# The clamp of the square sums on POOL, and the merge of the local heads with its addition ahead of the second maxima

## The chip, the cores and the metric

The kernel runs on one core of one Trainium2 chip. The time is that of the device for one execution, in microseconds (us). The core has five engines that run their own instruction streams and meet through semaphores: PE (TensorE, matmuls), DVE (VectorE), ACT (ScalarE), POOL (GpSimd) and SP (SyncE, which here only issues DMAs). PE writes to PSUM, POOL reads and writes only SBUF.

## The reference

The input is 16 sequences of 512 tokens with 128 channels. A first attention (16 heads of 8 channels, causal, with rotary positions) is added to the input. Then come two layers of a local transformer: 8 heads of 64 channels that look at their own and the previous window of 64 tokens, and a gated MLP. What bears on the change is the local attention's normalisation of queries and keys and what follows it:

```
def l2norm(t):
    return t / jnp.clip(jnp.linalg.norm(t, axis=-1, keepdims=True), 1e-12)
...
q = l2norm(q) * qs
k = l2norm(k) * ksc
q, k = rotary_xpos(q, k)
o = local_attention(q, k, v)
o = o.transpose(0, 2, 1, 3).reshape(b, n, INNER)
x = x + o @ wo
h = shift_token(x)
```

The kernel takes the norm as (max(sum of squares, 1e-24)) to the power -0.5. The maximum is "the clamp".

## The kernel before, in words

**Work and slots.** Two sequences (lanes) form a pair, and there are 8 pairs, numbered 0 to 7. The local layers work on tiles of 128 tokens: 2 layers x 2 lanes x 4 tiles = 16 tiles per pair, 128 in all. Each engine's program is a loop over slots `s` = 0 to 15 of a pair, written out by hand, and slot `s` holds work of several tiles in different stages: the local scores of tile `s`, the output projection ("merge") and the addition of tile `s-1`, the transposes of queries and keys of tile `s+1`, the rotation on POOL of tile `s+2` and the projection and square sums of tile `s+3`. Beside it the slot carries the first attention of a later pair. Two bodies ahead of pair 0 fill this pipeline; in pair 7 and the second half of pair 6 it runs dry.

**The first attention in a slot.** `attention_step(s, pos)` with `pos` 0 to 5 stands at six places of a slot on PE, DVE and ACT. On PE a step first issues the score matmuls from which DVE takes the row maxima (L587, into one PSUM bank), and then the score matmuls of a head six heads back, whose exponentials ACT takes (L600 and the mask L602, into another bank). There is one bank for each: L587 of a step waits until DVE has read the maxima of the step before (`maxed`), and L600 until ACT has read the step before (`exped`). The steps are 512, 384 + 128, 256 columns wide and then the same again. DVE reads the maxima at L977 (with a short read of the accumulator behind each). "The second maxima" are those of `pos` 1.

**The places that the change touches.**
- DVE, `norms(m)`: L1029 sums the squares of 16 heads (128x1024 to 128x16, `ss`), L1032 clamps them in place. L1029 waits for POOL's power of the tile before, since `ss` is one buffer.
- POOL, `over_norms(m)`: L1408 raises `ss` to -0.5 into `inv`, once DVE's L1012 (`unit_heads`, which writes `QN`) has used the old `inv`. Behind it stand the rotation L1386, L1397 (twice), L1403, then the normalisation of a tile for the MLP (L1378, L1414, L1417). In even slots the four small instructions of `maxima_parts` (L1367 to L1373) come first, for which PE waits with L622; in slots 1 and 9 `next_normalise` and in slots 7 and 15 `first_normalise` are added.
- ACT, `squares(m)`: L1221 writes `SQ` once the clamp of the tile before is done.
- PE, `merge(m)`: L786 multiplies the transposed heads `OT` (copied by ACT at L1235) by the output weights, into `m_ps`.
- DVE, `add_heads(m)`: L1048 adds the residual to it. When it is done, SP moves half of the channels by one token (`shift_tokens`, DMA `XN<-Z`), for which L1058 waits.
- Around them on PE: L699 projects queries and keys, L554 transposes (`turn_*`), L819 and L828 are matmuls of the MLP in even slots, L801 and L810 in odd ones, L751 applies the local weights, L725 and L734 are the local scores. On DVE L1076 multiplies the gates ahead of L828, L1039 divides the local output (`ON`), L949, L953 and L957 belong to the rotary embedding of the first attention, L1089 adds the last residual, L1019 and L1022 take the maxima of the local scores at the start of a slot.

Of the kernel before, what the change touches and what calls it, by code (L numbers as in the profile page):

```python
# [170 lines left out]
def build(nc, t, out):  # L171
    with ExitStack() as ctx:
# [218 lines left out]
        def past(sem, value):  # L391

            return (made, N_MADE) if isinstance(value, int) and value <= 0 else (sem, value)
# [153 lines left out]
        def _(pe):  # L547
# [28 lines left out]
            def body(i, slots):  # L576
# [76 lines left out]
                def attention_step(s, pos):  # L653
                    h, c = step_at(s, pos)
                    if s % 2 == 0 and pos == 2 and unit_in(i, s // 2 + 10):
                        turn_maxima(s, s // 2 + 10)
                    if s % 2 and pos == 0 and unit_in(i, (s + 17) // 2):
                        values(s, (s + 17) // 2)
                    if s % 2 and pos == 4 and unit_in(i, (s + 17) // 2):
                        heads_out((s + 17) // 2)  # L660
                    if head_in(i, h):
                        scores_max(h, c)
                    if head_in(i, h - BEHIND):
                        scores_exp(h - BEHIND, c)
# [172 lines left out]
                for s in slots:  # L837
                    z, two = s // 8, later(i, 2)
                    a = s % 2 and piece_in(i, (s - 3) // 2)
                    b = s % 2 == 0 and piece_in(i, (s - 4) // 2)  # L840
                    p = (s - 3) // 2 if s % 2 else (s - 4) // 2
                    if isinstance(i, int) and i == -2 and s == 8:
                        pe.wait_ge(consts, 16 * N_CONST)
                        for e in range(RING):
                            pe.wait_ge(*past(ones_in[e].sem, 16))
                    if tile_in(i, s):
                        scores(s)
                    attention_step(s, 0)
                    if tile_in(i, s - 1):
                        turn_o(s - 1)  # L850
                    if tile_in(i, s + 3):
                        project_qk(s + 3)
                    attention_step(s, 1)
                    if tile_in(i, s - 1):
                        merge(s - 1)
                    attention_step(s, 2)
                    if tile_in(i, s):
                        turn_p(s)
                    if a:
                        half_turn(p, s)  # L860
                    if b:
                        ups(p, s)
                    attention_step(s, 3)
                    if tile_in(i, s + 1):
                        turn_qk(s + 1)
                    if s % 8 == 2 and lives(i, 2):
                        maxima_over(s)
                        next_project(two, z, 0)
                    if s % 8 == 4 and lives(i, 2):
                        maxima_over(s)  # L870
                        next_project(two, z, 3)
                    if s % 8 == 6 and lives(i, 1):
                        merged_turn(z)
                    attention_step(s, 4)
                    if a:
                        gates(p)
                    if tile_in(i, s):
                        attend(s)
                    if b:
                        down(p)  # L880
                    if tile_in(i, s + 1):
                        project_v(s + 1)
                    if a:
                        last_chunk(p)
                    if s % 8 == 2 and lives(i, 2):
                        next_project(two, z, 1)
                    if s % 8 == 6 and lives(i, 1):
                        merged_project(z)
                    if s == 12 and lives(i, 1):
                        if lives(i, 2):  # L890
                            pe.wait_ge(*past(roped.sem[1], roped.at(two, 4)))
                        else:
                            maxima_over(s)
                        first_turn(0)
                    if b and half_of(p)[0] < L - 1:
                        turn_half(p)
                    attention_step(s, 5)
                    if s % 8 == 1 and lives(i, 2):
                        heads_over(s)
                        if z:  # L900
                            pe.wait_ge(*past(v1_ready.sem[0], v1_ready.at(two, 1)))
                        next_turn(two, z)
                    if s % 8 == 3 and lives(i, 2):
                        heads_over(s)
                        next_project(two, z, 2)
                    if s % 8 == 5 and lives(i, 2):
                        heads_over(s)
                        next_values(two, z)
                    if s == 15 and lives(i, 1):
                        heads_over(s)  # L910
                        first_turn(1)
# [4 lines left out]
        def _(v):  # L916
# [53 lines left out]
            def body(i, slots):  # L970
# [23 lines left out]
                def attention_step(s, pos):  # L994
                    h, c = step_at(s, pos)
                    if head_in(i, h):
                        row_maxima(h, c)
# [28 lines left out]
                def norms(m):  # L1026
                    v.wait_ge(*past(sq_done.sem, sq_done.at(i, m + 1)))
                    v.wait_ge(*past(inv_ready.sem, inv_ready.at(i, m)))
                    v.tensor_reduce(ss[:, :], SQ.rearrange("p (h e) -> p h e", e=E2), AX.X,  # L1029
                                    ALU.add).then_inc(ss_sum.sem, 1)  # L1030
                    v.wait_ge(*past(ss_sum.sem, ss_sum.at(i, m + 1)))
                    v.tensor_scalar(ss[:, :], ss[:, :], 1e-24, None, ALU.max).then_inc(ss_ready.sem, 1)  # L1032

                def over_sums(m):
                    v.wait_ge(*past(o_mm.sem, o_mm.at(i, m + 1)))
# [55 lines left out]
                for s in slots:  # L1091
# [13 lines left out]
                        next_low(two, z, 0)  # L1105
                    if s % 8 == 6 and lives(i, 2):
                        next_low(two, z, 1)
                    attention_step(s, 1)
                    if tile_in(i, s - 1):
                        add_heads(s - 1)  # L1110
                    attention_step(s, 2)
                    if s % 8 == 3 and lives(i, 2):
                        next_rest(two, z, 0)
# [38 lines left out]
        def _(a):  # L1152
# [20 lines left out]
            def body(i, slots):  # L1173
# [43 lines left out]

                def squares(m):
                    a.wait_ge(*past(raw_ready.sem, raw_ready.at(i, m + 1)))
                    a.wait_ge(*past(ss_ready.sem, ss_ready.at(i, m)))  # L1220
                    a.activation(SQ, RAW[m % 2], ACT.Square).then_inc(sq_done.sem, 1)  # L1221

                def exps(m):
# [102 lines left out]
        def _(g):  # L1326
# [32 lines left out]
            def body(i, slots):  # L1359
# [43 lines left out]
                    g.tensor_tensor(RC, RC, RS, ALU.add).then_inc(added.sem, 1)  # L1403

                def over_norms(m):
                    g.wait_ge(*past(ss_ready.sem, ss_ready.at(i, m + 1)))
                    g.wait_ge(*past(qn_ready.sem, qn_ready.at(i, m)))
                    g.tensor_tensor(inv[:, :], ss[:, :], nhalf[:, :], ALU.pow).then_inc(inv_ready.sem, 1)  # L1408
# [107 lines left out]
```

## Time and profile before

| | us |
|---|---|
| median of 3 runs | 2443.62 |
| the runs | 2433.88 to 2451.03 |
| the profiled execution | 2439.99 |
| its span | 2438.2 |

The granted clock of TensorE was 0.98 of full speed in the mean. The chain of work that ended last is spread over many lines, with 38% of the span on PE, 21% on DVE, 14% on ACT and 13% on POOL; no line has more than 4%. A slot takes 16.2 to 19.3 us in pair 2, and the pattern of slot lengths comes back every 16 slots (about 283 us). From 2200 us on slots of 12.7 and 14.5 us alternate.

How to read the rows: PE's matmuls are pipelined, so their durations overlap. A start less the start before it tells more than a duration. DVE's and ACT's rows overlap by some tenths for the same reason. "[0.51 <-DVE nmax L977]" behind a row is the time that the engine stood idle before it and what released it.

### The profile page before, as it was taken

What the parts mean: (1) busy time and instruction counts of PE and PEld (TensorE: products, weight loads), DVE (VectorE), ACT (ScalarE), POOL (GpSimd) and SP (SyncE); (2) the same over time, 40 slices, a digit from 0 to 9 for tenths busy, and PEclk for the clock granted to TensorE, in tenths of its full rate; (3) what the DMA queues carried; (4) which work ended last, traced back from release to release, by engine and by line L of the source; (5) the groups of instructions that cost most, each with busy time, mean ns of one, the idle gap of its engine ahead of it and who ended that gap; (6) DMA issues with size and microseconds to landing.
All of it is one profiled execution on the core that took longest, in us unless ns stands there. A gap on an engine that the chain in (4) does not pass through costs nothing.

```text
span 2438.2 us, 55022 instructions
## 1 busy us (share of the span) xinstructions
PE 2153.6 (88%) x20736; PEld 1447.8 (59%) x20736; DVE 1763.4 (72%) x4632; ACT 1553.0 (64%) x2510; POOL 1773.9 (73%) x1615
## 2 busy tenths in 40 slices
PE   4887899899999989998999999999899999988886
PEld 1444566665666666665666656666566666665654
DVE  4766777787777877788777777778777777666653
ACT  1445666676676667666766766766676667765553
POOL 2126768787777868787686777878787778788882
PEclk9999999999999999999999999999999999999997
DMA  4222121121212111121112112121121211111110
GB/s 138 65 66 54 40 53 49 44 59 45 57 37 60 52 46 49 48 59 46 49 49 59 44 45 58 33 64 51 39 51 47 60 48 36 25 32 27 28 25 23
DMA packets 115081, 119.56 MB, mean 49 GB/s; under 512 B 31945, under 2 KB 88054, under 8 KB 114818
## 3 DMA queue, kind: packets, MB, share of 16 engines
q1 hardware_dynamic: 114818, 116.04, 18.2%
q8 instruction: 167, 2.74, 0.5%
q14 instruction: 96, 0.79, 0.1%
HBM read 55.96 MB, written 20.97 MB: 32 GB/s over the span
## 4 chain that ended last, share of the span: by engine, by line
PE 38%; DVE 21%; ACT 14%; POOL 13%; issue 11%; DMA 1%; SPq 1%; ACTq 0%; DVEq 0%; POOLq 0%
PE ps L734 4%; PE ps L645 4%; POOL inv L1408 4%; DVE ps L977 4%; PE ps L554 4%; PE ps L828 3%; DVE nm L1019 3%; PE ps L587 3%; DVE ss L1029 3%; PE ps L712 3%; PE ps L600 2%; PE ps L567 2%; ACT PT L1190 2%; PE ps L810 2%; PE ps L819 2%
## 5 line engine op out<-in xcount | busy, mean ns | idle before, releaser
L977 DVE CUSTOM_DVE_ANT_0 ps<-ps,causal 128x512 f32<-128x512 f32 (+3 forms) x1024 | 492.4, 506 | 328.3 <-PE ps L587 322.3
L1408 POOL TENSOR_TENSOR inv<-ss,nhalf 128x16 f32<-128x16 f32 x128 | 377.7, 2950 | 394.0 <-DVE QN L1012 394.0
L1190 ACT ACTIVATE PT<-ps 128x512 f32<-128x512 f32 (+1 forms) x768 | 409.1, 536 | 352.5 <-PE ps L602 349.8
L587 PE MATMUL ps<-KA,QA 72*128 72x512 bf16 (+3 forms) x1024 | 275.1, 311 | 77.1 <-DVE nmax L977 72.9
L1397 POOL TENSOR_TENSOR RS<-RAW,rot 128x512 f32<-128x512 f32 x256 | 319.9, 1271 | 0.0
L1403 POOL TENSOR_TENSOR RC<-RC,RS 128x1024 f32<-128x1024 f32 x128 | 300.9, 2351 | 18.4
L600 PE MATMUL ps<-QA,KA 75*128 75x512 bf16 (+3 forms) x1024 | 286.8, 306 | 27.8 <-ACT PT L1190 26.0
L1386 POOL TENSOR_TENSOR RC<-RAW,rot 128x1024 f32<-128x1024 f32 x128 | 307.9, 2405 | 0.0
L1019 DVE TENSOR_REDUCE nm<-ps 128x8 f32<-128x1024 f32 x128 | 156.4, 1222 | 119.3 <-PE ps L734 119.3
L699 PE MATMUL ps<-wqkv,ZT 128*128 128x512 f32 x512 | 241.9, 595 | 0.0
L587 PEld LDWEIGHTS ps<-KA,QA 72*128 72x128 bf16 x1024 | 96.4, 100 | 235.3 <-DVE nmax L977 142.4
L1249 ACT COPY V_odd<-ps 128x512 f32<-128x512 f32 x128 | 75.0, 586 | 233.6 <-PE ps L712 232.1
L1029 DVE TENSOR_REDUCE ss<-SQ 128x16 f32<-128x1024 f32 x128 | 155.7, 1217 | 72.5 <-POOL inv L1408 65.5
L602 PE MATMUL ps<-causal_t,identb 128*128 128x128 bf16 x1024 | 200.9, 222 | 0.0
L1225 ACT ACTIVATE PX<-PX 128x1024 f32<-128x1024 f32 x128 | 136.5, 1067 | 54.8 <-DVE PX L1022 54.1
L600 PEld LDWEIGHTS ps<-QA,KA 75*128 75x128 bf16 x1024 | 101.0, 99 | 115.8 <-ACT PT L1190 64.7
L645 PE MATMUL ps<-PT,V 128*32 128x512 f32 (+3 forms) x2048 | 153.4, 440 | 9.1 <-DVE X L1003 2.9
L1022 DVE TENSOR_TENSOR PX<-ps,nm 128x1024 f32<-128x1024 f32 x128 | 156.7, 1224 | 4.4
L1012 DVE TENSOR_TENSOR QN<-RC,inv 128x1024 f32<-128x1024 f32 x128 | 156.5, 1223 | 0.0
L828 PE MATMUL ps<-w,G 128*128 128x128 f32 (+1 forms) x768 | 110.8, 297 | 44.8 <-DVE G L1076 44.8
L734 PEld LDWEIGHTS ps<-KT,QT 64*64 64x64 f32 x4096 | 114.3, 136 | 56.7 <-issue 56.7
L751 PE MATMUL ps<-V_even,PT 128*64 128x65 f32 x2048 | 147.2, 225 | 0.4
(122 smaller groups left out, 5304.9 us busy)
## 6 DMA issues: line engine op xcount, KB each, us to landing
V_even<-V_odd SPq DMA_DIRECT2D x256, 130.0 KB, 2.6
QA<-parts SPq DMA_DIRECT2D x192, 96.0 KB
KA<-parts SPq DMA_DIRECT2D x192, 96.0 KB
parts<-qkp SPq DMA_DIRECT2D x32, 384.0 KB, 3.5
X_next<-in_x SPq DMA_DIRECT2D x16, 256.0 KB, 3.1
X<-in_x SPq DMA_DIRECT2D x16, 256.0 KB, 2.9
x_kept<-X SPq DMA_DIRECT2D x16, 256.0 KB, 3.8
XR<-x_kept SPq DMA_DIRECT2D x32, 128.0 KB, 2.9
```

What stands on the lines that cost most here:

```text
L587: last = pe.matmul(dst[:, c0:c0 + w], QA[e][0:QK_ROWS, h % UNIT, qt * P:(qt + 1) * P], KA[e][0:QK_ROWS, h % UNIT, 0:w], start=True, stop=True)
L600: pe.matmul(dst[:, c0:c0 + w], KA[e][0:ROWS, h % UNIT, kt * P:(kt + 1) * P], QA[e][0:ROWS, h % UNIT, kt * P:S], start=True, stop=False)
L645: last = pe.matmul(a_ps[32 * n:32 * (n + 1), kt * P:S], V1[z][:, kt, h * VW:h * VW + 32], PT1[:, n, c0:c0 + w], start=(kt == 0), stop=(kt ...
L699: mm = pe.matmul(ps[:, w, :], ZT[z][:, tt * P:(tt + 1) * P], wqkv[:, l, w * INNER:(w + 1) * INNER], start=True, stop=True)
L977: ins = v.tensor_tensor_reduce(for_max(i, x)[:, c0:c0 + w], for_max(i, x)[:, c0:c0 + w], causal[:, S - w:S], -1.0, -NEG, ALU.add, ALU.min, ...
L1019: v.tensor_reduce(nm[:, :], blocks, AX.X, ALU.max, negate=True).then_inc(max_ready.sem, 1)
L1029: v.tensor_reduce(ss[:, :], SQ.rearrange("p (h e) -> p h e", e=E2), AX.X, ALU.add).then_inc(ss_sum.sem, 1)
L1190: a.activation(PT1[:, h % UNIT, c0:c0 + w], for_exp(i, x)[:, 0:w], ACT.Exp, scale=SCALE1).then_inc(exped.sem, 1)
L1386: g.tensor_tensor(RC.rearrange(heads, w=2, h=H2), RAW[m % 2].rearrange(heads, w=2, h=H2), rot[:, l, tt, 0, :, :].unsqueeze(2).to_broadcast ...
L1397: ins = g.tensor_tensor(turned[:, w, :, :, :], by_half[:, w, :, :, :], table[:, w, :, :].unsqueeze(1).to_broadcast([P, H2, 2, E2 // 2]), A ...
L1403: g.tensor_tensor(RC, RC, RS, ALU.add).then_inc(added.sem, 1)
L1408: g.tensor_tensor(inv[:, :], ss[:, :], nhalf[:, :], ALU.pow).then_inc(inv_ready.sem, 1)
```

## The change

The clamp moves from DVE's `norms` to POOL's `over_norms`, ahead of the power. It waits for the sum, and ACT's `squares` now waits for the sum too. PE's `merge(s - 1)` moves from behind `attention_step(s, 1)` to ahead of it, and DVE's `add_heads(s - 1)` does the same.

```
@@ PE, the loop over slots
-                    attention_step(s, 1)
                     if tile_in(i, s - 1):
                         merge(s - 1)
+                    attention_step(s, 1)
                     attention_step(s, 2)
@@ DVE, norms(m)
                     v.tensor_reduce(ss[:, :], SQ.rearrange("p (h e) -> p h e", e=E2), AX.X,
                                     ALU.add).then_inc(ss_sum.sem, 1)
-                    v.wait_ge(*past(ss_sum.sem, ss_sum.at(i, m + 1)))
-                    v.tensor_scalar(ss[:, :], ss[:, :], 1e-24, None, ALU.max).then_inc(ss_ready.sem, 1)
@@ DVE, the loop over slots
-                    attention_step(s, 1)
                     if tile_in(i, s - 1):
                         add_heads(s - 1)
+                    attention_step(s, 1)
                     attention_step(s, 2)
@@ ACT, squares(m)
-                    a.wait_ge(*past(ss_ready.sem, ss_ready.at(i, m)))
+                    a.wait_ge(*past(ss_sum.sem, ss_sum.at(i, m)))
@@ POOL
                 def over_norms(m):
+                    g.wait_ge(*past(ss_sum.sem, ss_sum.at(i, m + 1)))
+                    g.tensor_scalar(ss[:, :], ss[:, :], 1e-24, None, ALU.max).then_inc(ss_ready.sem, 1)
                     g.wait_ge(*past(ss_ready.sem, ss_ready.at(i, m + 1)))
```

The lines between the removed and the added ones of DVE and POOL move up by two in the changed kernel (L1048 becomes L1046). On PE, in an even slot, these are the instructions between the transposes of `ON` and the maxima of step 2, before:

```order
L554 MATMUL ps<-ident,ON 128x128 x4
L699 MATMUL ps<-wqkv,ZT 128x512 x2
L587 MATMUL ps<-KA,QA 128x384
L587 MATMUL ps<-KA,QA 128x128
L600 MATMUL ps<-QA,KA 128x384
L602 MATMUL ps<-causal_t,identb 128x128
L600 MATMUL ps<-QA,KA 128x128
L602 MATMUL ps<-causal_t,identb 128x128
L786 MATMUL ps<-wo,OT 128x128 x4
L622 MATMUL ps<-identb,nparts 128x128 x4
L587 MATMUL ps<-KA,QA 128x256
```

And now:

```order
L554 MATMUL ps<-ident,ON 128x128 x4
L699 MATMUL ps<-wqkv,ZT 128x512 x2
L786 MATMUL ps<-wo,OT 128x128 x4
L587 MATMUL ps<-KA,QA 128x384
L587 MATMUL ps<-KA,QA 128x128
L600 MATMUL ps<-QA,KA 128x384
L602 MATMUL ps<-causal_t,identb 128x128
L600 MATMUL ps<-QA,KA 128x128
L602 MATMUL ps<-causal_t,identb 128x128
L622 MATMUL ps<-identb,nparts 128x128 x4
L587 MATMUL ps<-KA,QA 128x256
```

The merge (L786) no longer stands between the maxima of step 1 and those of step 2. In an odd slot L622 is not there, and only L600 and L602 are left between them.

On POOL, from the small instructions of `maxima_parts` to the rotation, before:

```order
L1371 TENSOR_TENSOR nparts<-nres,unit 128x4x4
L1373 TENSOR_TENSOR nparts<-nres,nparts 128x4x4
L1408 TENSOR_TENSOR inv<-ss,nhalf 128x16
L1386 TENSOR_TENSOR RC<-RAW,rot 128x1024
L1397 TENSOR_TENSOR RS<-RAW,rot 128x8x2x32 x2
```

And now:

```order
L1369 TENSOR_TENSOR nparts<-nres,unit 128x4x4
L1371 TENSOR_TENSOR nparts<-nres,nparts 128x4x4
L1405 TENSOR_SCALAR ss<-ss 128x16
L1408 TENSOR_TENSOR inv<-ss,nhalf 128x16
L1384 TENSOR_TENSOR RC<-RAW,rot 128x1024
L1395 TENSOR_TENSOR RS<-RAW,rot 128x8x2x32 x2
```

The clamp (now L1405) stands directly ahead of the power, in front of the power's wait for `QN`.

## Rows read from the trace of the kernel before

**Rows 1.** The page: busy us (share of the span) and instructions of each engine
```profile
PE 2153.6 (88%) x20736; PEld 1447.8 (59%) x20736; DVE 1763.4 (72%) x4632; ACT 1553.0 (64%) x2510; POOL 1773.9 (73%) x1615
```

**Rows 2.** Groups by line: busy us, mean ns, idle before and releaser
```profile
L1408 POOL TENSOR_TENSOR inv<-ss,nhalf 128x16 f32<-128x16 f32 x128 | 377.7, 2950 | 394.0 <-DVE QN L1012 394.0
...
L1032 DVE TENSOR_SCALAR ss<-ss 128x16 f32<-128x16 f32 x128 | 119.3, 932 | 4.4
...
L1048 DVE TENSOR_TENSOR Z<-ps,Z 128x128 f32<-128x128 f32 x64 | 18.5, 290 | 21.2 <-PE ps L786 21.2
...
L1367 POOL TENSOR_TENSOR nparts<-nmax,unit 128x16 bf16<-128x16 f32 x64 | 13.7, 215 | 107.3 <-DVE nmax L977 107.3
```

**Rows 3.** The line of the clamp alone: ns min/median/max, first and last start
```profile
L1032 DVE TENSOR_SCALAR ss<-ss x128: 175/878/3462, 192.8 to 2364.7; 128x16 f32<-128x16 f32 x128
```

**Rows 4.** Waits: who waited for whom, us in total, times, longest
```profile
POOL inv L1408 <- DVE QN L1012: 394.0, 92, 8.6
```

**Rows 5.** Timeline, slot 14 of pair 2: start, us, engine, instruction [idle before]
```profile
1048.02 1.22 DVE L1032 TENSOR_SCALAR ss<-ss 128x16 f32<-128x16 f32 x1
...
1047.93 2.50 POOL L1397 TENSOR_TENSOR RS<-RAW,rot 128x512 f32<-128x512 f32 x2
...
1050.19 1.60 PE L828 MATMUL ps<-w,G 128*128 128x128 f32 x12 [0.84 <-DVE G L1076]
```

**Rows 6.** Timeline, slot 1 of pair 2, DVE, POOL and PE
```profile
816.22 3.46 DVE L1032 TENSOR_SCALAR ss<-ss 128x16 f32<-128x16 f32 x1
...
817.15 2.50 POOL L1397 TENSOR_TENSOR RS<-RAW,rot 128x512 f32<-128x512 f32 x2
...
821.49 0.28 PE L587 MATMUL ps<-KA,QA 72*128 72x256 bf16 x1 [1.66 <-DVE nmax L977]
```

**Rows 7.** Timeline, slot 13 of pair 2 (odd), PE, then DVE, then ACT
```profile
1024.86 0.22 PE L602 MATMUL ps<-causal_t,identb 128*128 128x128 bf16 x1
1024.92 1.11 PE L786 MATMUL ps<-wo,OT 128*128 128x128 f32 x8
1025.87 0.27 PE L587 MATMUL ps<-KA,QA 72*128 72x256 bf16 x1
1026.43 0.28 PE L600 MATMUL ps<-QA,KA 75*128 75x256 bf16 x1 [0.29 <-ACT PT L1190]
...
1024.78 0.57 DVE L977 CUSTOM_DVE_ANT_0 ps<-ps,causal 128x384 f32<-128x384 f32 x1 [0.82 <-PE ps L587]
...
1025.51 0.14 DVE L977 DVE_READ_ACCUMULATOR2_ANT nmax<- 128x1 f32 x1
...
1025.74 0.63 ACT L1190 ACTIVATE PT<-ps 128x512 f32<-128x512 f32 x1
```

**Rows 8.** The chain that ended last, the same slot: start, us, what
```profile
1026.43 0.28 PE ps L600
```

**Rows 9.** Timeline, slot 10 of pair 2, DVE, then PE
```profile
970.97 0.14 DVE L977 DVE_READ_ACCUMULATOR2_ANT nmax<- 128x1 f32 x1
...
971.17 0.28 PE L587 MATMUL ps<-KA,QA 72*128 72x256 bf16 x1
```

**Rows 10.** Timeline, slot 12 of pair 2, DVE, then POOL
```profile
1013.80 2.33 DVE L949 TENSOR_TENSOR rope_t<-rope_t,rope_s 128x512 f32<-128x512 f32 x1
...
1013.23 2.35 POOL L1403 TENSOR_TENSOR RC<-RC,RS 128x1024 f32<-128x1024 f32 x1
```

**Rows 11.** Timeline, slot 8 of pair 2, DVE, then PE
```profile
942.50 0.65 DVE L1032 TENSOR_SCALAR ss<-ss 128x16 f32<-128x16 f32 x1
943.07 0.21 DVE L1058 BATCH_NORM_STATS2 stats<-XN 128x6 f32<-128x64 f32 x1
...
944.11 1.60 PE L828 MATMUL ps<-w,G 128*128 128x128 f32 x12 [0.71 <-DVE G L1076]
```

**Rows 12.** Late slots: a piece of the chain (the clamp), then a row of POOL's timeline
```profile
2253.12 0.77 issue
...
2303.12 2.92 POOL L1408 TENSOR_TENSOR inv<-ss,nhalf 128x16 f32<-128x16 f32 x1
```

More of the change, by code:

```diff
@@ L852, in body @@
                         project_qk(s + 3)
-                    attention_step(s, 1)
                     if tile_in(i, s - 1):
                         merge(s - 1)
+                    attention_step(s, 1)
                     attention_step(s, 2)
@@ L1030, in norms @@
                                     ALU.add).then_inc(ss_sum.sem, 1)
-                    v.wait_ge(*past(ss_sum.sem, ss_sum.at(i, m + 1)))
-                    v.tensor_scalar(ss[:, :], ss[:, :], 1e-24, None, ALU.max).then_inc(ss_ready.sem, 1)
                 def over_sums(m):
@@ L1107, in body @@
                         next_low(two, z, 1)
-                    attention_step(s, 1)
                     if tile_in(i, s - 1):
                         add_heads(s - 1)
+                    attention_step(s, 1)
                     attention_step(s, 2)
@@ L1219, in squares @@
                     a.wait_ge(*past(raw_ready.sem, raw_ready.at(i, m + 1)))
-                    a.wait_ge(*past(ss_ready.sem, ss_ready.at(i, m)))
+                    a.wait_ge(*past(ss_sum.sem, ss_sum.at(i, m)))
                     a.activation(SQ, RAW[m % 2], ACT.Square).then_inc(sq_done.sem, 1)
@@ L1405, in over_norms @@
                 def over_norms(m):
+                    g.wait_ge(*past(ss_sum.sem, ss_sum.at(i, m + 1)))
+                    g.tensor_scalar(ss[:, :], ss[:, :], 1e-24, None, ALU.max).then_inc(ss_ready.sem, 1)
                     g.wait_ge(*past(ss_ready.sem, ss_ready.at(i, m + 1)))
```

## The prediction

> **What bounds the kernel now.** The page comes first. PE is busy 88% of the span, and DVE, POOL and ACT 64 to 73% [rows 1], so no engine is full and each slot has its own last wait. A slot is the stretch between two starts of DVE's L1019. The reader should then look at the clamp, L1032. It handles 128x16 elements, yet it takes 932 ns in the mean [rows 2] and anything from 175 to 3462 ns [rows 3]. Its length depends on what it runs into. In slot 14 it starts at 1048.02 and ends at 1049.24, about where the first of POOL's two RS instructions ends (2.50 us from 1047.93, so half of it at 1049.18) [rows 5]. In slot 1 it starts at 816.22 and ends at 819.68, when POOL's RS pair, begun at 817.15, ends at 819.65 [rows 6]. So the clamp waits for POOL to let go, sometimes for one instruction and sometimes for three.
>
> The Trainium skill (SBUF — State Buffer, "SBUF: two separate sides") says that DVE and GpSimd share a port pair that one instruction holds to its end while the other blocks. Slot 14 agrees. In slot 1 the rule would free the clamp at 817.15, where RS begins, so the clamp would cost 0.93 us there, and taking it away could return no more than that instead of the 1.66 used below. The forecast would be 6 x 0.73 = 4.4 us higher, 2441.7.
>
> The chain of waits then says which slots feel DVE at all. In the odd slots but 1 and 7 it runs through ACT, whose exponentials follow PE's scores [rows 7, 8]. In slots 2 and 10 it runs through PE. In slots 6, 8 and 14 it runs through L1029, L1032, L1058 and the gates into PE's L828. In slots 7 and 8 POOL is the chain until PE's L622.
>
> **Change 1, the clamp leaves DVE.** DVE loses 128 x 932 ns = 119 us of busy time [rows 2], but only what a waiting engine gets counts. I take it by slot, for one pair (16 slots).
> - Slot 1: the clamp holds DVE for 3.46 us, and PE stands idle 1.66 us ahead of L587 because of it [rows 6]. PE can recover no more than that: 1.66.
> - Slots 6 and 14: the clamp costs 1.1 us, but PE's idle time ahead of L828 is 0.84 [rows 5]: 0.84 each, 1.68 (slot 6 repeats the pattern of 14).
> - Slot 8: 0.57 from the clamp's start (942.50) to that of L1058 (943.07), less than PE's idle 0.71 [rows 11]: 0.57.
> - Slots 0, 4 and 12: some 0.2 each. In slot 12 it goes nowhere: L949, which reads two SBUF tensors, waits until POOL's L1403 is over (15.58) and ends at 16.13, whenever it came [rows 10]. POOL's place there is set by QN, ahead of both edits. I take slots 0 and 4 alike: 0.
> - Slots 2 and 10 and the other odd ones: PE or ACT is the chain: 0.
>
> Gain per pair 1.66 + 1.68 + 0.57 = 3.9 us. The full pattern runs in pairs 0 to 5: 23.4 us.
>
> In the end of the program (from 2088 us, without the first attention's maxima) POOL and DVE alternate on the chain. In nine even slots the clamp stands on it with 0.9 us, from 2133 to 2365 us; its longest piece, here at 2253.12, is 0.77 [rows 12].
>
> **Change 2, the clamp on POOL.** The trace has no such instruction. Two rows of the same 128x16 shape on POOL bound it: 215 ns for a multiplication and 2950 ns for the power [rows 2]. Since a maximum is simple arithmetic, I take the first, with 0.08 of waiting for its own semaphore: 0.3. Where POOL waits for QN ahead of the power, which happens 92 of 128 times and 394 us in all [rows 4], the clamp runs inside that wait, since the sums were ready one slot earlier. If that cover were gone, it would cost 0.3 x 92 = 28 us at most. In 36 slots POOL does not wait, as at 2303.12 [rows 12]. The nine late slots are among them, where power, sums and gates follow each other: 0.9 - 0.3 = 0.6 each, a gain of 5.4 us. In slot 1 the 0.3 lies within the 1.8 us that PE's idle time leaves of the clamp's 3.46. The new wait on `ss_sum` holds up the power and the rotation behind it, but the sum comes before it by nearly a slot. ACT's squares wait for the sum instead of the clamp, and that was never their last wait.
>
> **Change 3, the merge ahead of the second maxima on PE.** The merge takes 0.95 us of PE (1024.92 to 1025.87) [rows 7]. In an odd slot PE comes to this place without a pause. Before, the scores of step 1 ended at 1025.08, and ACT, busy until about 1025.8, took them at 1025.74 [rows 7]. Now they end at 1026.03, so ACT loses 0.3. The larger loss is the next step. L587 of step 2 waits until DVE has read step 1 out of the same bank. That read took 0.87 (1024.78 to 1025.65), and the merge used to cover it. Now the read starts 0.95 later, at 1025.73, and ends at 1026.60; L587 starts at 1026.68 and L600 behind it at 1026.80, against 1026.43 [rows 7]. This L600 stands on the chain [rows 8]: +0.37, and ACT runs without a pause after it, so it goes through. That makes six slots (3, 5, 9, 11, 13, 15) x 0.37 = 2.2. In slot 1 QN delays DVE anyway: +0.28. In slot 7 POOL covers it: 0.
>
> In an even slot PE waits 0.5 ahead of step 1 and the merge fills part of that, but DVE is later still.
>
> **Change 4, the addition ahead of the second maxima on DVE.** It takes 0.29 [rows 2], some 0.25 from start to start. In slot 10 step 1 is read until 971.11 and PE starts step 2 at 971.17 [rows 9], so the two meet with nothing to spare and the addition puts PE back by 0.25. The same holds for slots 2, 6 and 14: 1.0 per pair. In 0, 4 and 12 it is absorbed like the gain, and in 8 POOL covers it. The tokens get to SP's queue earlier by 0.3 to 0.8, but DVE hardly waits for that shift. Cost of changes 3 and 4 per pair: 2.2 + 0.28 + 1.0 = 3.5, over six pairs 21.0, and in the thinner pair 6 1.5 (slots 1, 3 and 5 at 0.37, and 0.4 for the even ones).
>
> **Sum.** -23.4 - 5.4 + 21.0 + 1.5 = -6.3 us. The profiled execution took 2439.99 (span 2438.2), 3.6 under the median of the runs, 2443.62. Against the median: **2437.3 us**, 0.3% less.
>
> **The rivals.**
> - A, the gain alone: the moved merge costs nothing, since PE and ACT make up 0.4 us elsewhere in the slot. For it: PE has idle time in each slot. Against it: in the odd slots it lies ahead of the chain. 2443.6 - 23.4 - 5.4 = 2415.
> - B, the stall moves on (the slower side): the other DVE instructions with two SBUF inputs, L949 and L1089, now start a little earlier against POOL's row of instructions and miss a hand-over as the clamp did in slot 1. If one of them per pair waits 3.46 more [rows 6], that is 6 x 3.46 = 20.8: 2437.3 + 20.8 = 2458. It decides from 1.05 us per pair on (6.3 / 6). Against it: DVE arrives there within 0.1 of its old time, since gain and cost cancel.
> - C, the cost alone: PE's idle times of [rows 5, 6] have a second cause right behind the clamp, so the 23.4 and the 5.4 fail and the cost stays, with 0.3 x 9 for the clamp on POOL: 2443.6 + 22.5 + 2.7 = 2469.
> - D, the clamp is as slow on POOL as the power: 2.65 more in six slots 1 and nine late ones: 2437.3 + 15 x 2.65 = 2477. Against it: 215 ns for four other kinds of simple arithmetic of this shape.
>
> **Numbers.** The forecast gets 0.50, A 0.14, B 0.14, C 0.08, D 0.04; 0.10 is left for what I do not see, on both sides. Own range of the forecast: 2428 to 2446. Over all cases: 2418 to 2462, which leaves out most of A, C and D. A measurement of this kernel tells about 1% from no change, that is 2419 and 2468. Faster by over 1% 0.13 (nearly all of A), slower by over 1% 0.10 (D and half of C), within 1% 0.77.
>
> **What would show it.** In the profile after: DVE busy 119 us less; a clamp of about 0.2 us on POOL; slot 1 shorter by 1.4 us; PE's waits for DVE ahead of L828 nearly gone; but PE waiting ahead of step 2 for DVE in the odd slots, and ACT's exponential of step 2 about 0.4 us later after slot start. The forecast is wrong if the odd slots keep their length (A), or if L949 or L1089 grow in the mean (B).

## The result and the profile after

| | before | after |
|---|---|---|
| median of four runs each, us | 2447.32 | 2417.89 |
| lowest to highest | 2433.88 to 2452.00 | 2410.79 to 2421.13 |
| profiled execution (span) | 2439.99 (2438.2) | 2418.14 (2416.4) |

The ratio is 0.9885, with a 95% interval of 0.9838 to 0.9932: 1.15% faster. On the chip of the first experiments it was 0.9844 (0.9813 to 0.9876). The forecast of 2437.3, 0.3% faster, had the direction but a quarter of the size. It was worked out from a median of 2443.62, without the fourth run of the kernel before (2452.00). The time lies outside the forecast's own range (2428 to 2446), 0.1 under the lower end of the range over all cases (2418 to 2462) and next to rival A. A gain of over 1% had been given a chance of 0.13.

The page after, busy us of each engine, answers to [rows 1]:

```profile
PE 2140.1 (89%) x20736; PEld 1463.9 (61%) x20736; DVE 1698.7 (70%) x4504; ACT 1561.1 (65%) x2510; POOL 1826.3 (76%) x1743
```

DVE has 128 instructions less but only 65 us less to do, not 119. POOL has 52 us more. The groups by line (busy us, mean ns, idle before and releaser) answer to [rows 2]:

```profile
L1408 POOL TENSOR_TENSOR inv<-ss,nhalf 128x16 f32<-128x16 f32 x128 | 378.7, 2959 | 324.6 <-DVE QN L1012 320.0
...
L953 DVE TENSOR_TENSOR rope_s<-rope_t,qkp 128x512 f32<-128x512 f32 x32 | 66.4, 2074 | 1.4 <-ACT qkp L1160 1.4
...
L1405 POOL TENSOR_SCALAR ss<-ss 128x16 f32<-128x16 f32 x128 | 40.0, 313 | 0.0
```

And the clamp's line alone (ns min/median/max), which answers to [rows 3]:

```profile
L1405 POOL TENSOR_SCALAR ss<-ss x128: 247/256/1225, 197.5 to 2351.8; 128x16 f32<-128x16 f32 x128
```

The clamp takes 0.26 us on POOL in the median, near the 0.22 of a multiplication. Eight of the 128 take 1.1 to 1.2, so the mean is 0.31. Of the 55 us of DVE time that did not vanish, 44 have gone to L953, which reads two SBUF tensors: it took 0.69 us before and now takes 2.07 in the mean. L1089 (now L1087) has grown from 1.07 to 1.32 in the mean, 8 us in all, and L949 has shrunk from 1.34 to 1.21.

Slot 1 of pair 2 after (timeline, start, us; DVE, POOL, then PE) answers to [rows 6]:

```profile
809.05 1.22 DVE L1029 TENSOR_REDUCE ss<-SQ 128x16 f32<-128x1024 f32 x1 [1.18 <-POOL inv L1408]
810.19 0.22 DVE L1056 BATCH_NORM_STATS2 stats<-XN 128x6 f32<-128x64 f32 x1
...
805.69 0.25 POOL L1405 TENSOR_SCALAR ss<-ss 128x16 f32<-128x16 f32 x1
806.02 2.93 POOL L1408 TENSOR_TENSOR inv<-ss,nhalf 128x16 f32<-128x16 f32 x1
...
813.58 0.28 PE L587 MATMUL ps<-KA,QA 72*128 72x256 bf16 x1
```

L1056 (L1058 before) follows the sum at once where 3.46 us lay between. PE's L587 has lost its idle time of 1.66. The power starts 0.33 after the clamp does. PE's idle time ahead of L828 in slots 6, 8 and 14 of this pair is gone too. Over the whole trace PE's wait for the gates ahead of L828 is halved and not nearly gone, 21.4 us after 44.8.

Slot 13 of pair 2 after (PE, DVE, ACT) answers to [rows 7]:

```profile
1016.91 1.05 PE L786 MATMUL ps<-wo,OT 128*128 128x128 f32 x8
1017.80 0.38 PE L587 MATMUL ps<-KA,QA 72*128 72x384 bf16 x2
...
1019.20 0.28 PE L587 MATMUL ps<-KA,QA 72*128 72x256 bf16 x1 [0.68 <-DVE nmax L977]
1019.32 0.28 PE L600 MATMUL ps<-QA,KA 75*128 75x256 bf16 x1
...
1018.08 0.29 DVE L1046 TENSOR_TENSOR Z<-ps,Z 128x128 f32<-128x128 f32 x1 [1.56 <-PE ps L786]
1018.28 0.56 DVE L977 CUSTOM_DVE_ANT_0 ps<-ps,causal 128x384 f32<-128x384 f32 x1
...
1019.87 2.61 DVE L953 TENSOR_TENSOR rope_s<-rope_t,qkp 128x512 f32<-128x512 f32 x1
...
1018.57 0.60 ACT L1188 ACTIVATE PT<-ps 128x512 f32<-128x512 f32 x1
```

This is the new wait of the prediction's change 3. The second L587 now waits 0.68 us for DVE, where the merge stood before. The chain that ended last (start, us, what) runs through it:

```profile
1017.08 0.91 PE ps L786 x8
...
1018.08 0.29 DVE Z L1046
1018.37 0.47 DVE ps L977
...
1019.20 0.30 PE ps L587
```

Merge, addition, maxima of step 1, matmuls of step 2: each waits for the one before it. Over the whole trace the waits of PE for DVE's maxima (us, times, longest) have grown, before and after:

```profile
PE ps L587 <- DVE nmax L977: 72.9, 116, 3.9
...
PE ps L587 <- DVE nmax L977: 111.8, 147, 1.7
```

The slots of pair 1, in us between two starts of L1019, from the timelines of four kernels (two of them are experiments below):

```
slot            0    1    2    3    4    5    6    7    8    9   10   11   12   13   14   15   sum
before       16.6 17.8 16.5 18.2 19.3 18.5 18.4 16.2 17.6 17.3 16.5 18.4 18.8 18.5 18.2 16.6 283.5
after        16.6 16.0 16.6 18.7 19.4 18.8 17.7 16.6 16.5 17.4 16.7 18.8 18.6 18.8 17.6 16.8 281.4
clamp only   15.2 16.9 17.3 18.1 19.4 18.5 17.5 16.2 17.2 17.0 16.6 18.5 18.5 18.5 17.6 16.3 279.3
moves only   16.6 17.4 17.0 18.8 19.4 18.8 18.4 16.6 17.0 17.7 17.2 18.8 18.8 18.8 18.2 16.9 286.3
```

The change shortens slots 1, 6, 8 and 14 and lengthens the other odd ones by 0.1 to 0.5, 2.1 us less in all (in pair 2: 283.1 to 282.0, from the starts 783.38 and 1065.34 of after). Yet the two traces differ by 21.8 us in span. The rest lies in single pairs: 5.2 us in pair 0, 6.1 in pair 3, 2.4 in pair 4, 2.3 in pair 6, 3.9 in pair 7.

Two things set the longer pairs of the kernel before apart. In slot 15 of pair 3 a clamp takes 3.45 us, as in the slots 1; and TensorE's clock falls more often in some pairs. It is granted at 1.00 of full speed (2.4 GHz) for most of the time and falls to 0.50 (1.2 GHz) for stretches of 3.4 us, some of them twice as long. These rows show slot 4 of pair 3 and slot 4 of pair 4 in the trace before. First come the two windows with their length, the busy time of each engine and the granted clock (the third figure from the end), and then PE's rows:

```profile
1161.00:1165.00 4.00, 4.00 (x49) 2.04 (x42) 3.67 (x5) 0.96 (x3) 0.00 (x0) 1.00 0.03 10
1448.40:1451.70 3.30, 3.30 (x40) 1.75 (x40) 1.46 (x2) 0.87 (x2) 0.00 (x0) 0.50 0.26 90
...
1160.03 1.10 PE L734 MATMUL ps<-KT,QT 64*64 64x128 f32 x32
1161.06 2.36 PE L645 MATMUL ps<-PT,V 128*32 128x512 f32 x32
...
1448.21 1.94 PE L734 MATMUL ps<-KT,QT 64*64 64x128 f32 x32
1450.08 3.15 PE L645 MATMUL ps<-PT,V 128*32 128x512 f32 x32
```

The first slot takes 19.3 us and the second 20.2. Here are the eight pairs of four kernels (16 slots, 15 in pair 7), in us, with the number of stretches at half clock that begin there in brackets:

```
pair             0          1          2          3          4          5          6          7
before       282.0 (2)  283.5 (0)  283.1 (0)  287.4 (1)  285.7 (2)  283.3 (0)  256.3 (2)  211.5 (4)
after        276.8 (1)  281.4 (1)  282.0 (1)  281.3 (1)  283.3 (1)  283.5 (1)  254.0 (1)  207.6 (5)
clamp only   274.3 (0)  279.3 (0)  280.7 (1)  279.6 (0)  279.6 (0)  280.3 (0)  252.7 (1)  204.8 (4)
moves only   286.2 (3)  286.3 (0)  290.2 (2)  289.4 (1)  291.6 (3)  287.6 (2)  262.3 (2)  207.1 (2)
```

Each of the seven stretches in pairs 0 to 6 of the trace before comes with, or a few us behind, an idle time of PE of 1.65 to 3.88 us. Three of the seven follow a clamp of 3.45 us: in slot 1 of pair 0, in slot 15 of pair 3 and in slot 1 of pair 4. The same idle time does not always bring one. In both slots 4 above, PE stood idle for 2.35 us shortly ahead of L734. Nor does each stretch cost time: that of pair 1 after leaves slot 4 at 19.4 us.

### The profile page after: what moved, and what is told of

Same layout as the page of the kernel before. It is cut to its first block, busy times and chain, and to the rows that moved or that the text cites. A ratio compares the mean times of both kernels' runs of the same rounds, so it can differ in the third digit from the quotient of the medians.

```text
span 2416.4 us, 55022 instructions
## 1 busy us (share of the span) xinstructions
PE 2140.1 (89%) x20736; PEld 1463.9 (61%) x20736; DVE 1698.7 (70%) x4504; ACT 1561.1 (65%) x2510; POOL 1826.3 (76%) x1743
## 4 chain that ended last, share of the span: by engine, by line
PE 50%; DVE 20%; POOL 14%; issue 10%; ACT 4%; DMA 1%; SPq 0%; DVEq 0%; POOLq 0%; ACTq 0%
DVE ps L977 6%; PE ps L554 6%; PE ps L645 5%; PE ps L734 4%; PE ps L751 4%; PE ps L587 4%; PE ps L712 4%; PE ps L828 3%; DVE nm L1019 3%; POOL inv L1408 3%; PE ps L699 3%; PE ps L600 3%; PE ps L567 2%; PE ps L819 2%; PE ps L810 2%
## 5 line engine op out<-in xcount | busy, mean ns | idle before, releaser
L587 PE MATMUL ps<-KA,QA 72*128 72x512 bf16 (+3 forms) x1024 | 274.7, 310 | 113.7 <-DVE nmax L977 111.8
L1395 POOL TENSOR_TENSOR RS<-RAW,rot 128x512 f32<-128x512 f32 x256 | 330.1, 1311 | 0.0
L1384 POOL TENSOR_TENSOR RC<-RAW,rot 128x1024 f32<-128x1024 f32 x128 | 302.7, 2365 | 0.0
L600 PE MATMUL ps<-QA,KA 75*128 75x512 bf16 (+3 forms) x1024 | 285.5, 304 | 10.6 <-ACT PT L1188 9.0
L1019 DVE TENSOR_REDUCE nm<-ps 128x8 f32<-128x1024 f32 x128 | 156.3, 1221 | 112.3 <-PE ps L734 112.2
L587 PEld LDWEIGHTS ps<-KA,QA 72*128 72x128 bf16 x1024 | 99.3, 100 | 208.8 <-DVE nmax L977 145.5
L602 PE MATMUL ps<-causal_t,identb 128*128 128x128 bf16 x1024 | 200.7, 222 | 0.0
L786 PEld LDWEIGHTS ps<-wo,OT 128*128 128x128 f32 x1024 | 134.1, 191 | 63.0 <-issue 57.4
L645 PE MATMUL ps<-PT,V 128*32 128x512 f32 (+3 forms) x2048 | 161.3, 458 | 8.5 <-ACT PT L1188 2.3
L600 PEld LDWEIGHTS ps<-QA,KA 75*128 75x128 bf16 x1024 | 101.2, 99 | 81.2 <-ACT PT L1188 27.4
L554 PE MATMUL ps<-ident,PX 128*128 128x128 f32 x1024 | 138.5, 280 | 12.1 <-ACT PX L1223 12.1
```

Source lines behind the costliest of these rows:

```text
L554: last = pe.transpose(dst[:, tt * P:(tt + 1) * P], src(tt), ident[:, :])
L587: last = pe.matmul(dst[:, c0:c0 + w], QA[e][0:QK_ROWS, h % UNIT, qt * P:(qt + 1) * P], KA[e][0:QK_ROWS, h % UNIT, 0:w], start=True, stop=True)
L600: pe.matmul(dst[:, c0:c0 + w], KA[e][0:ROWS, h % UNIT, kt * P:(kt + 1) * P], QA[e][0:ROWS, h % UNIT, kt * P:S], start=True, stop=False)
L645: last = pe.matmul(a_ps[32 * n:32 * (n + 1), kt * P:S], V1[z][:, kt, h * VW:h * VW + 32], PT1[:, n, c0:c0 + w], start=(kt == 0), stop=(kt ...
L1384: g.tensor_tensor(RC.rearrange(heads, w=2, h=H2), RAW[m % 2].rearrange(heads, w=2, h=H2), rot[:, l, tt, 0, :, :].unsqueeze(2).to_broadcast ...
L1395: ins = g.tensor_tensor(turned[:, w, :, :, :], by_half[:, w, :, :, :], table[:, w, :, :].unsqueeze(1).to_broadcast([P, H2, 2, E2 // 2]), A ...
```

## The experiments

All times are medians of the runs of one kernel, all ratios are against runs of the kernel before on the same chip. Experiments of one group shared a chip.

**Apart: the clamp and the moves.** The first kernel is the change without these two edits; the second is the kernel before with these two alone.

```
-                    attention_step(s, 1)
                     if tile_in(i, s - 1):
                         merge(s - 1)
+                    attention_step(s, 1)
...
-                    attention_step(s, 1)
                     if tile_in(i, s - 1):
                         add_heads(s - 1)
+                    attention_step(s, 1)
```

> Only the clamp moves to POOL (with ACT's changed wait); merge and addition stay behind the second maxima. The theory of the prediction (the clamp gains, the moves cost 3.5 us per pair): 21 us faster than the whole change, some 2400 us, ratio to before 0.978 to 0.983, and the odd slots 3, 5, 11 and 13 keep the 18.5 us or less of before. The rival (the moves are free or help): equal to the whole change, ratio 0.988 and above.

> Only the merge on PE and the addition on DVE move ahead of the second maxima; the clamp stays on DVE. The theory: 20 us slower than before, ratio 1.006 to 1.011, with PE waiting for DVE ahead of L587 in the odd slots 0.4 us longer. The rival (the moves are free or help): ratio 0.995 to 1.002.

> The whole change once more, on the chip of the other runs, to compare with them: both theories expect its first ratio again, 0.984 to 0.993.

Measured: the clamp only 2404.37 us, ratio 0.9799 (0.9770 to 0.9828); the moves only 2468.36, ratio 1.0070 (1.0044 to 1.0096); the whole change 2415.94, ratio 0.9844; before 2450.15. So the clamp brings 46 us and the moves take 18 where the clamp is on DVE and 12 where it is on POOL. The theory that the moves cost stands, and rival A, in which they are free, falls. The whole change is 12 us slower than its first half alone, where 21 were expected. Slots 3, 5, 11 and 13 keep their length with the clamp only, 18.1 to 18.5, and grow by 0.3 to 0.6 with the moves only. Waits in the second kernel:

```profile
PE ps L587 <- DVE nmax L977: 120.8, 150, 3.6
```

**The clamp's own cost on POOL.** On the order of the kernel with the clamp only:

```
 def over_norms(m):
     g.wait_ge(*past(ss_sum.sem, ss_sum.at(i, m + 1)))
-    g.tensor_scalar(ss[:, :], ss[:, :], 1e-24, None, ALU.max).then_inc(ss_ready.sem, 1)
-    g.wait_ge(*past(ss_ready.sem, ss_ready.at(i, m + 1)))
```

> Merge and addition as before, and no clamp at all: the maximum of the square sums with 1e-24 is left out of the computation, and the power follows the sum at once. It measures the clamp's own cost on POOL against the kernel with only the clamp moved. The theory (0.3 us, hidden in POOL's wait for QN in most slots): 3 to 6 us faster than that kernel. The rival (the clamp's wait and dispatch on POOL cost in every slot): 20 us or more faster than it.

Measured: 2393.07 us, ratio 0.9754 (0.9726 to 0.9782), 11 us faster than with the clamp on POOL. Both expectations missed: it is more than 3 to 6, and less than 20. One more kernel, meant to clamp and raise to the power in one instruction on POOL, gave no time. To see whether the clamp's length is what counts, the next one has it twice:

```
     g.tensor_scalar(ss[:, :], ss[:, :], 1e-24, None, ALU.max).then_inc(ss_ready.sem, 1)
+    g.wait_ge(*past(ss_ready.sem, ss_ready.at(i, 2 * m + 1)))
+    g.tensor_scalar(ss[:, :], ss[:, :], 1e-24, None, ALU.max).then_inc(ss_ready.sem, 1)
```

> The kernel with only the clamp moved, with the clamp twice on POOL, the second waiting for the first. The kernel without a clamp was 11 us faster than the one with it on POOL. The theory (0.34 us per clamp in the slots where POOL is late, the cause of those 11): 8 to 15 us slower than with one clamp, ratio 0.983 to 0.986. The rival (the 11 us came from how POOL's and DVE's instructions happen to meet, not from the clamp's length): within 4 us of one clamp or faster.

Measured: 2423.13 us, ratio 0.9892 (0.9866 to 0.9918), 19 us slower than with one (2404.37 on another chip; by the ratios 0.9% or 23 us). So the clamp's length does count. It seems to count more than in proportion, against 8 to 15 us expected, but 11 and 19 to 23 us are only about as far apart as the intervals of the ratios allow. POOL did not wait for QN in 56 of 128 slots of the kernel with the clamp only, not in 36 as in [rows 4]: with the faster DVE, POOL is late more often.

```profile
POOL inv L1408 <- DVE QN L1012: 303.1, 72, 8.2
```

The traces show where the clamp's length counts by itself. An even slot of pair 7 that has no half-clock stretch in any of the three traces (slot 10) takes 13.5 us without a clamp on POOL, 13.8 with one and 14.1 with two. That is 0.3 for each clamp. The larger part of the difference is again the clock: pair 7 takes 195.7 us in the kernel without a clamp, with no half-clock stretch in its slots, and 204.8 with the clamp only, with four. In pairs 0 to 6 these two traces differ by 4 us the other way, with six stretches without a clamp and two with it. Why the clock falls less often late in the one kernel and more often earlier is not shown.

**Is it DVE's work or the wait for POOL?** The kernel before with another instruction for the clamp on DVE, in the same place:

```
-    v.tensor_reduce(ss[:, :], SQ.rearrange("p (h e) -> p h e", e=E2), AX.X,
+    v.tensor_reduce(ssp[:, :, 0], SQ.rearrange("p (h e) -> p h e", e=E2), AX.X,
                     ALU.add).then_inc(ss_sum.sem, 1)
     v.wait_ge(*past(ss_sum.sem, ss_sum.at(i, m + 1)))
-    v.tensor_scalar(ss[:, :], ss[:, :], 1e-24, None, ALU.max).then_inc(ss_ready.sem, 1)
+    v.tensor_reduce(ss[:, :], ssp[:, :, :], AX.X, ALU.max).then_inc(ss_ready.sem, 1)
```

> The kernel before, but DVE clamps with another instruction: the sums are written beside a constant 1e-24 and a TENSOR_REDUCE takes the larger of each two (128x16x2 to 128x16), in the place of the TENSOR_SCALAR. Order and waits are unchanged. The theory (what costs is that the TENSOR_SCALAR waits for POOL's instructions, not that DVE clamps): the new instruction takes 0.2 us in every slot and never waits for POOL, and the time is that of the kernel with only the clamp moved within 8 us, ratio 0.977 to 0.984. The rival (any instruction of DVE there waits, or the gain comes from DVE's program being shorter): 0.9 us in the mean and a ratio of 0.995 to 1.002.

Measured: 2402.4 us against 2450.9, ratio 0.9790 (0.9766 to 0.9815). The groups by line of this kernel:

```profile
L1033 DVE TENSOR_REDUCE ss<-ssp 128x16 f32<-128x32 f32 x128 | 23.8, 186 | 4.4
```

The same work on twice the elements takes 186 ns in the mean instead of 932, and 189 at most. DVE clamps in the same place behind the same waits, and the whole gain of moving the clamp is there. So what cost was the form of the instruction, which waits for POOL, and not that DVE did it.

**Which of the two moves costs?** With the clamp on POOL, first only PE's merge moves, then only DVE's addition.

> The clamp on POOL, PE's merge ahead of the second maxima, but DVE's addition behind them as before. The theory gives the merge 0.37 us in six odd slots, and the addition 0.25 in four even ones: this kernel lies 7 to 14 us over the one with only the clamp moved and 3 to 6 us under the whole change, ratio 0.981 to 0.984. The rival (the addition is what costs, since DVE waits for the merge ahead of it): equal to the kernel with only the clamp moved, 0.980.

> The clamp on POOL, DVE's addition ahead of the second maxima, but PE's merge behind its matmuls of that step as before. DVE then waits for the whole merge ahead of the maxima of step 1, and PE for these ahead of step 2, so the merge covers nothing either. The theory: as long as or up to 15 us longer than the whole change, ratio 0.984 to 0.992, with DVE idle ahead of the addition. The rival (only PE's order counts): 0.980.

Measured: merge moved 2413.05 us, ratio 0.9840 (0.9820 to 0.9861); addition moved 2468.36, ratio 1.0069 (1.0049 to 1.0089). The merge alone carries 0.4%, or 10 us, which is all or nearly all of the cost. The addition behind it adds 1 us by the ratios and 3 by the medians, which the runs don't tell from 0 or from the 3 to 6 expected. The addition alone was expected at up to 15 us over the whole change and came out about 50 over it. Slot 13 of pair 2 of that kernel, DVE and then PE:

```profile
1020.64 0.28 DVE L1046 TENSOR_TENSOR Z<-ps,Z 128x128 f32<-128x128 f32 x1
1020.85 0.55 DVE L977 CUSTOM_DVE_ANT_0 ps<-ps,causal 128x384 f32<-128x384 f32 x1
...
1019.08 1.11 PE L786 MATMUL ps<-wo,OT 128*128 128x128 f32 x8
1021.76 0.28 PE L587 MATMUL ps<-KA,QA 72*128 72x256 bf16 x1 [1.10 <-DVE nmax L977]
```

DVE's maxima now stand behind PE's merge, which stands behind PE's own step 1: PE waits 1.1 us ahead of step 2, against 0.68 in the whole change, and in nearly every slot (225 waits of its weight loads against 160).

**Is L953's stall part of the cost?** The whole change, with L953 ahead of `unit_heads`:

```
+                    if s % 8 == 3 and lives(i, 2):
+                        next_rest(two, z, 0)
+                    if s % 8 == 5 and lives(i, 2):
+                        next_rest(two, z, 1)
                     if tile_in(i, s + 1):
                         unit_heads(s + 1)
```

> The whole change, and DVE's L953 (rope_s, two SBUF inputs, slots 3, 5, 11, 13) ahead of unit_heads instead of behind the second step's maxima. In the whole change L953 takes 2.6 us in the middle, against 0.69 before, since it meets POOL's rotation. The theory (PE's wait ahead of step 2 is the whole cost of the moves, and that stall is hidden behind ACT): the time of the whole change within 4 us. The rival (the stall of L953 is a good part of the cost): 5 to 10 us faster than the whole change, ratio 0.980 to 0.983.

Measured: 2420.78 us against 2452.16, ratio 0.9883 (0.9857 to 0.9909); the whole change had 0.9844 and 0.9885. L953 is back at 0.69 us in every slot and nothing is gained. In pair 1 slots 3, 5, 11 and 13 take 18.7, 18.8, 18.8 and 18.8 us in both traces, though in the changed kernel the chain of slot 13 runs through L953 with 1.03 us. In that slot of pair 2 ACT has no pause of over 0.05 us between 7.8 us after its start (the exponential of step 2) and 15.2, so the stall, from 8.0 to 10.6, lies beside a full ACT and is hidden. The earlier place may cost something of its own, which no run takes apart: QN comes later, and POOL's wait for it is 334.6 us instead of 320.0.

**No clamp instruction at all.** Square leaves a 65th column for each head, and the guard 1e-24 stands there as a constant from the start, so that the sum includes it (it is added, not the larger of two). On the order of the kernel with the clamp only, and then with the moves:

```
-    a.activation(SQ, RAW[m % 2], ACT.Square).then_inc(sq_done.sem, 1)
+    a.activation(SQ[:, :, 0:E2], RAW[m % 2].rearrange("p (h e) -> p h e", e=E2),
+                 ACT.Square).then_inc(sq_done.sem, 1)
...
+    g.memset(SQ[:, :, E2:E2 + 1], 1e-24).then_inc(made, 1)
```

> Merge and addition as before. No clamp instruction: the squares get a 65th column per head that holds 1e-24, and L1029 sums it too, so the power sees sum + 1e-24 instead of max(sum, 1e-24). The theory: as the kernel without a clamp, 2393 us within 5, ratio 0.975 to 0.978, the best so far. A rival: ACT's write of 64 of 65 columns is slower, or the sum over 1040 elements collides anew, and nothing is left against the clamp on POOL (0.980).

> The kernel with the constant column, and merge and addition ahead of the second maxima. It measures the two moves where no clamp stands on any engine. The theory: 11 to 22 us slower than the same kernel without the moves, ratio 0.980 to 0.985, since the cost lies in PE's wait ahead of step 2. The rival (the moves cost only where the clamp has been shifted about): within 5 us.

Measured: 2394.91 us, ratio 0.9780 (0.9753 to 0.9808), and with the moves 2406.81, ratio 0.9823 (0.9797 to 0.9848). The first has the lowest time here that keeps a guard against a zero sum, 0.7 to 1.1% under the change itself by the ratios (0.9844 and 0.9885); the sum takes 1233 ns for 1040 elements instead of 1215. It is not told apart from the clamp by TENSOR_REDUCE (0.9790). The moves cost 12 us here too, so the cost does not depend on a clamp instruction.

**The kernel before once more,** for a second trace.

> The kernel before once more, for a second trace of it. Its runs spread over 27 us (2435 to 2462), those with the clamp off DVE over 8. The theory (the spread and the part of the gain that the prediction missed come from further hits of the clamp's wait, where POOL happens to be late): this trace has clamps of over 3 us outside slot 1 of a pair, at other places than the first trace, and its slots there are 2 us or more longer; ratio 1.00. The rival (the spread comes from the clock or the DMAs, everywhere alike): the clamps over 3 us are the same seven, and all slots stretch a little.

Measured: 2449.28 us, ratio 1.0005 (0.9985 to 1.0024). Nine clamps take over 3 us here: the six of slot 1 and three more, at 678.86, 1248.88 and 1642.87. The first trace had seven, the six and one at 1350.99. The last of the three, DVE and then POOL:

```profile
1641.61 1.22 DVE L1029 TENSOR_REDUCE ss<-SQ 128x16 f32<-128x1024 f32 x1 [1.88 <-POOL inv L1408]
1642.87 3.45 DVE L1032 TENSOR_SCALAR ss<-ss 128x16 f32<-128x16 f32 x1
...
1641.48 2.36 POOL L1386 TENSOR_TENSOR RC<-RAW,rot 128x1024 f32<-128x1024 f32 x1
1643.81 2.48 POOL L1397 TENSOR_TENSOR RS<-RAW,rot 128x512 f32<-128x512 f32 x2
```

It is the pattern of slot 1 in slot 15 of pair 4. POOL is late, the sum is released by the power, and the clamp falls behind L1386 and does not get its turn before L1397 ends (1646.29). That slot takes 19.5 us instead of 16.6. The one in slot 15 of pair 3 of the first trace took 20.8, and there the clock fell behind the stall:

```profile
1356.20:1359.50 3.30, 3.24 (x25) 2.22 (x29) 1.48 (x5) 1.54 (x3) 3.06 (x8) 0.50 0.00 0
...
1356.26 0.39 PE L587 MATMUL ps<-KA,QA 72*128 72x256 bf16 x1 [2.52 <-DVE nmax L977]
```

The other two cost less than the 2 us expected: slot 9 of pair 1 takes 17.7 instead of 17.3. Both stand one slot behind a half-clock stretch in slot 8, which takes 18.8 us instead of 17.6. Slot 4 takes 20.8 instead of 19.3 in three pairs of this trace, each time with such a stretch, and 20.6 to 21.1 with one in four pairs of the kernel without any clamp. So the stalls do wander, and so do the stretches at half clock, which need no clamp.

The rival, that the spread comes from the clock, was set aside too soon. Both traces of this kernel are among its fastest executions (2440 us), but the mean granted clock is on record for every run. In this group it is 0.981 for the run of 2440.42 and 0.970 for that of 2468.72. In the first group the four slowest runs of this kernel (2458 to 2462) have 0.972 and the three fastest (2435 to 2444) 0.977 to 0.980. The runs with the clamp only have 0.979 to 0.987. From 0.981 to 0.972, 22 us of full clock are missing, or 44 us at half clock, 13 stretches of 3.4 us. One cost 0.9 to 1.6 us in slots 4 and in the late slots, where it showed, so that is up to 12 to 21 us by estimate, and such runs lie 19 us apart. Whether the clock makes a run long, or a run with longer waits of PE gets less clock, these runs don't separate.

## Why the prediction was right or wrong

- **What bounds the kernel, and the clamp's wait for POOL: right.** The experiment with TENSOR_REDUCE shows it. In slot 1 the clamp waits beyond the end of the POOL instruction it first met, and the second trace shows the same at another place. The rule of the Trainium skill (SBUF — State Buffer, "SBUF: two separate sides") is that one instruction holds the port pair to its end while the other side blocks. The prediction read it so that the clamp would come up at 817.15, where L1386 ends. It ended at 819.68, so that reading fails; the rule itself does not say which side gets the pair next, and the trace does not contradict it.
- **Change 1, the gain per slot: right in the main.** With the clamp only, pair 1 is 4.2 us shorter, against 3.9 forecast, and neither trace has a half-clock stretch there. Slots 6, 8 and 14 gain 0.9, 0.4 and 0.6 (0.84, 0.57 and 0.84 forecast), and 0 to 2 together 1.5 (1.66). That makes 3.4 of the 4.2. Slots 9, 12 and 15, which stood at 0, gain 0.3 each.
- **The step that failed is the multiplication.** The gain was taken from one undisturbed pair for all six, and 0 was taken for pair 6. By the traces, pairs 0 to 5 gained 31.2 us instead of 23.4 (pairs 0, 3 and 4 alone 21.6), pair 6 3.6 instead of 0, and the two medians differ by 46 where 28.8 was the forecast (23.4 and 5.4). Pairs 0, 3 and 4 are the ones in which the trace before has its five half-clock stretches and the clamp of 3.45 us in slot 15, and the trace with the clamp only has none there. The sum had no term for either: it took TensorE's clock as the same before and after. The last 4 us between the traces (41.5) and the medians (46) stay open, and so does the clock's share in the 46. The median granted clock of the runs rose from 0.976 to 0.981, by the same estimate up to 6 to 11 us.
- **The late slots: right only at full clock.** Slots of 14.5 became 13.8 us with the clamp on POOL: 0.7 instead of the 0.6 forecast. But slots 4 and 8 of pair 7, 14.5 before, take 15.4 to 15.5 in both traces with the clamp on POOL, each with a half-clock stretch that they did not have. Pair 7 as a whole is 6.7 us shorter with the clamp only and 3.9 with the whole change (5.4 forecast for the late slots). On POOL the clamp stands as forecast: 0.26 us, 0.33 from start to start.
- **Change 2, the cost on POOL: too low.** Without the clamp on POOL the kernel is 11 us faster still. The sum had it only in the late slots and slot 1. There it costs the 0.3 forecast; the rest goes with the number of half-clock stretches in pair 7 and is not explained.
- **Change 3, the merge: right, mechanism and size.** The chain runs through merge, addition, maxima and L587. Against the kernel with the clamp only, the six odd slots of pair 1 are 2.4 us longer in all, and with the moves only 2.2 longer than before (2.2 forecast). In slot 5 of pair 2 L600 of step 2 starts 7.23 us after the start of the slot instead of 6.89 (0.37 forecast) and ACT's exponential 7.60 instead of 7.27.
- **Change 4, the addition in even slots: wrong in its slots.** 0.25 in each of slots 2, 6, 10 and 14 was forecast. In pair 1 they are together 0.4 shorter than with the clamp only. With the moves only, slots 2 and 10 are 0.55 and 0.77 longer than before, and 6 and 14 not at all. L587 of step 2 does come 0.2 later in slot 14 after its start (5.86 instead of 5.67), but what follows in PE's row takes it up, just as it kept the gain there at 0.6. In slot 8, put at 0, the moves save 0.7. In pair 1 both moves cost 2.1 with the clamp on POOL and 2.8 with it on DVE, instead of 3.5. In the medians they cost 12 us instead of 22.5 with the clamp on POOL.
- **The net, -6.3, was a difference of two terms of over 20 us,** and both errors went the same way: 17 us too little gain and 11 too much cost. That the time still came out at the range's edge is due to the width of the range, and the size of the net was not foreseen.
- **The rivals.** A had the right time, but its reason is refuted. B, a stall that moves on, is real, and by its own sign, since L1089 did grow in the mean (1.07 to 1.32), though most of it hit L953 (0.69 to 2.07), which B had not named. It did not make the kernel slower than forecast, and without L953's stall nothing was gained. C and D fell: PE's idle times of [rows 5, 6] were gone, and 0.26 us is far from the 2.95 of the power.

## What to carry to other kernels

When the duration of an instruction varies by a factor of 20 with one shape, suspect a wait that the profile books as busy time, as it did here. Look at what the other engine does at its end, and try another form of the same instruction before moving it to another engine. And when a matmul is moved out from between two steps that share a PSUM bank, the reader of that bank loses its cover: here 10 us, more than a fifth of what the other half of the change had won. Before multiplying the gain of one slot pattern by the number of its repeats, compare the repeats, and look at the granted clock of those that differ.

## What the runs showed of the hardware

- A 128x16 TENSOR_SCALAR in SBUF on DVE took 175 to 3462 ns beside POOL's stream, a TENSOR_REDUCE of 128x32 in its place 185 to 189. The same TENSOR_SCALAR on POOL took 247 to 1225.
- The waiting DVE instruction did not always get its turn when POOL's instruction ended. In slot 1 and at 1642.87 it was passed over between L1386 and L1397 and between the two of L1397, and came up only where POOL itself paused, 0.14 us ahead of L1403. In slot 14 it did come up between the two of L1397 (1049.24).
- Two-input instructions of DVE in SBUF (L953, L949, L1089) show the same stretching: L953 and L949 took 0.69 to 2.9 us and L1089 0.42 to 2.6. Which of them is hit changed with shifts of some tenths of a microsecond.
- TensorE's granted clock fell from 1.00 to 0.50 for 3.4 us at a time, with or just behind idle times of PE of 1.65 us and more, and not behind each of them. At 0.50 the 32 matmuls of L734 took 1.94 us instead of 1.10.
